# A Flamingo layer on one core: rows stored tile by tile on Pool, selection ahead of the row extreme, and half of the softmax exponentials straight from PSUM on ACT

## The reference, cut to what matters

```python
# x (2,1024,256), ctx (2,64,256); 16 heads of 64; 8 experts of width 192, top 2
q = einsum('bsd,dhf->bshf', layernorm(x), Wq) + bq;  q = q / sqrt(64)
k, v = ctx @ Wk + bk, ctx @ Wv + bv                  # 64 keys per batch
probs = softmax(einsum('bqhf,bkhf->bhqk', q, k), axis=-1)
x = x + tanh(g_xattn) * (einsum(probs, v) @ Wo + bo)
y = layernorm(x)
scores = sigmoid(y @ W_router)
_, sel = top_k(scores + expert_bias, 2)
w = scores[sel] / (sum + 1e-20)
out = silu(y @ Wg_s) * (y @ Wu_s) @ Wd_s             # shared expert
out += sum over the 2 chosen e of w_e * (silu(y @ Wg[e]) * (y @ Wu[e]) @ Wd[e])
x = x + tanh(g_ffn) * out
```

## Time and profile before

| | us |
|---|---|
| median of 3 runs | 340.79 |
| lowest, highest | 337.12, 341.66 |
| the profiled execution | 341.64 |
| its span in the trace | 339.9 |
| granted TensorE clock, mean | 0.925 |

### The profile page before, as it was taken

The page is one execution under the profiler, slowest core; times in us unless marked ns, Lnnn a source line. Parts: engine busy times, 40 slices in busy tenths (PEclk is TensorE's granted clock), DMA queues, the critical chain, the costliest instruction groups (busy, mean ns, idle before and its releaser), DMA issues.

```text
span 339.9 us, 6401 instructions
## 1 busy us (share of the span) xinstructions
PE 287.4 (85%) x1792; PEld 259.9 (76%) x1793; DVE 254.9 (75%) x672; ACT 143.3 (42%) x349; POOL 161.2 (47%) x208
## 2 busy tenths in 40 slices
PE   3968979999989989969678848798999999999660
PEld 2957768999978888959577748697898989999440
DVE  1687898999999998869785673269766667776586
ACT  1471653555655655635353323543344344444100
POOL 7022023356638888884876554029343434343400
PEclk9997998999999999979987996789999999999755
DMA  6790003011112222211100144023333343331768
GB/s 189 276 355 12 0 0 95 1 48 47 49 46 78 95 93 79 74 53 48 63 32 33 47 156 145 16 66 94 96 108 111 84 122 96 114 105 43 243 220 278
DMA packets 28892, 33.23 MB, mean 98 GB/s; under 512 B 3688, under 2 KB 25538, under 8 KB 28866
## 3 DMA queue, kind: packets, MB, share of 16 engines
q1 hardware_dynamic: 22706, 21.82, 21.5%
q0 software_dynamic: 3408, 8.46, 7.1%
q10 hardware_dynamic: 2752, 2.63, 2.4%
HBM read 21.14 MB, written 12.67 MB: 99 GB/s over the span
## 4 chain that ended last, share of the span: by engine, by line
PE 52%; DVE 21%; POOL 10%; issue 8%; ACT 3%; DMA 3%; SPq 1%; DVEq 0%; POOLq 0%; ACTq 0%
PE bank L1234 9%; PE bank L1236 8%; PE bank L1235 8%; PE scores_ps L1234 6%; PE scores_ps L1235 5%; PE scores_ps L1236 5%; POOL rows_dram L544 4%; DMA x_sb<-in_x_dram 3%; PE bank L1382 3%; POOL probs L573 2%; PE bank L1221 2%; DVE probs L1052 2%; DVE row_sum L1030 2%; DVE pT_lo L1025 2%; DVE x_sb L1144 2%
## 5 line engine op out<-in xcount | busy, mean ns | idle before, releaser
L624 POOL DMA_INDIRECT routed_dram<-probs,sct_idx x39 | 38.4, 986 | 68.8 <-DVE probs L1131 67.2
L1236 PE MATMUL bank<-AB_hi,pT_lo 128*128 128x256 f32 (+1 forms) x206 | 59.4, 289 | 0.0
L573 POOL TENSOR_TENSOR probs<-probs,row_inv 128x1024 f32<-128x1024 f32 x16 | 30.5, 1904 | 35.1 <-DVE row_inv L1034 35.1
L1236 PEld LDWEIGHTS bank<-AB_hi,pT_lo 128*128 128x128 f32 (+1 forms) x206 | 40.8, 198 | 0.0
L1234 PE MATMUL bank<-AB_hi,pT_hi 128*128 128x256 f32 x128 | 39.1, 306 | 0.0
L1235 PE MATMUL bank<-AB_lo,pT_hi 128*128 128x256 f32 x128 | 37.7, 295 | 0.0
L544 POOL DMA_INDIRECT rows_dram<-xn,slot_i x32 | 31.9, 996 | 11.3 <-issue 8.9
L1234 PE MATMUL scores_ps<-AB_hi,xnT_hi 128*128 128x512 f32 x64 | 26.4, 412 | 3.2 <-DVE xnT_lo L1014 3.2
L1234 PE MATMUL bank<-AB_hi,pT_lo 96*128 x78 | 25.2, 323 | 2.0 <-DVE pT_lo L1134 1.9
L1234 PEld LDWEIGHTS bank<-AB_hi,pT_hi 128*128 128x128 f32 x128 | 26.4, 206 | 0.1
L1235 PEld LDWEIGHTS bank<-AB_lo,pT_hi 128*128 128x128 f32 x128 | 26.1, 204 | 0.1
(11 more groups left out here) (222 smaller groups left out, 839.7 us busy)
## 6 DMA issues: line engine op xcount, KB each, us to landing
probs<-rows_dram SPq DMA_DIRECT2D x30, 130.0 KB, 2.2
x_sb<-in_x_dram SPq DMA_DIRECT2D x2, 1024.0 KB, 9.6
AB_free<-routed_dram SPq DMA_DIRECT2D x4, 512.0 KB, 5.6
AB_free<-routed_dram SPq DMA_DIRECT2D x8, 256.0 KB, 4.6
out_dram<-x_sb ACTq DMA_DIRECT2D x8, 256.0 KB, 2.2
raw_buf<-in_L_ffn_Wg_dram SPq DMA_DIRECT2D x8, 192.0 KB, 2.5
raw_buf<-in_L_ffn_Wu_dram SPq DMA_DIRECT2D x8, 192.0 KB, 3.0
raw_buf<-in_L_ffn_Wd_dram SPq DMA_DIRECT2D x4, 384.0 KB, 3.5
```

The source lines that it names most:

```text
L573: nc.gpsimd.tensor_tensor(pr, pr, row_inv[:, :].unsqueeze(2).to_broadcast([P, H, KV]), ALU.mult).then_inc(norm_done, 1)
L624: nc.gpsimd.indirect_dma_start(routed_dram[:, :], bass.IndirectOffsetOnAxis(ap=sct_idx[(k - 2) % (2 * RING)][:, 0:1], axis=0), y_sb[ks][:, ...
L1236: return nc.tensor.matmul(out_ap, a_lo, b_hi, start=False, stop=last)
```

## The change

Four things are edited.

1. POOL: `put_batch` with its table of parts becomes `put_tile(t)`, one tile (two indirect stores) a step from step 6 on, placed right after the second layernorm and **ahead of** the normalisation of the probabilities; steps 14 and 15 store two tiles each.
2. DVE: `choose` moves from behind the subtraction to in front of the row extreme.
3. The sign of the scores is turned in the folded weights, so that the row extreme is a minimum, `neg_max`. For heads 0 to 7, ACT now reads `scores_ps` itself, with `exp(-s + neg_max)`, one activation of 64 columns for each head, whose accumulator output gives that head's row sum (`direct_exponentials`, signal `direct_done`). Heads 8 to 15 keep the old way: subtraction on DVE (512 columns), exponential on ACT (512 columns), sum on DVE (512 columns). The next tile's scores wait for `direct_done` too.
4. ACT's list: the exponential stands behind `xnT_hi` in all steps, `W_hi` in front of `xn2T_hi`, and the eight new activations behind `xn2T_hi` and in front of `AB_hi`.

```diff
@@ POOL
-            def put_batch(b, part=slice(None)):
-
+            def put_tile(t):
+
+                b = [t < z for _, z in BATCHES].index(True)
                 pool.wait_ge(slot_done, b + 1)
                 pool.wait_ge(payload_done, b + 1)
-                for t in list(range(*BATCHES[b]))[part]:
-                    put_rows(t)
+                put_rows(t)
...
                 if inside(w):
                     second_norm(w)
+                if 6 <= t < T:
+                    put_tile(t - 6 if t < T - 2 else 2 * t - 20)
                 if inside(m):
...
-                if t == 6:
-                    put_batch(0, slice(0, 1))
-                if t == 7:
-                    put_batch(0, slice(1, 2))
-                if t == 8:
-                    put_batch(0, slice(2, 4))
...
-                if t == 12:
-                    put_batch(2, slice(0, 2))
...
+                if T - 2 <= t < T:
+                    put_tile(2 * t - 19)
@@ ACT
-                                         scale=DH ** -0.5, bias=q_beta[:, c:c + 1]).then_inc(wqT_done, 1)
+                                         scale=-DH ** -0.5, bias=q_beta[:, c:c + 1]).then_inc(wqT_done, 1)
...
                 def exponentials():
                     act.wait_ge(sub_done, m + 1)
-                    nc.scalar.activation(prob[1 - q][:, :], prob[1 - q][:, :], ACT.Exp).then_inc(exp_done, 1)
-
-                if inside(m) and not scores_first:
-                    exponentials()
+                    nc.scalar.activation(prob[1 - q][:, HK // 2:], prob[1 - q][:, HK // 2:], ACT.Exp, scale=-1.0).then_inc(exp_done, 1)
+
+                def direct_exponentials():
+                    act.wait_ge(max_done, u + 1)
+                    after(act, pT_done, 2 * t + 2)
+                    for h in range(H // 2):
+                        heads = slice(h * KV, (h + 1) * KV)
+                        e = nc.scalar.activation(prob[q][:, heads], scores_ps[:, heads], ACT.Exp, scale=-1.0,
+                                                 bias=neg_max[:, h:h + 1], accum_out=row_sum[:, h:h + 1])
+                    e.then_inc(direct_done, 1)
+
                 if inside(u):
...
+                if inside(m) and not scores_first:
+                    exponentials()
                 if folding:
...
                 if inside(w):
                     second_norm(w)
-                    high_xn2(w, 1 - q)
                 if 2 <= t < 2 + E:
...
+                if inside(w):
+                    high_xn2(w, 1 - q)
+                if inside(u):
+                    direct_exponentials()
                 if 2 + E <= t < 6 + E:
@@ DVE
-                    nc.vector.tensor_reduce(row_sum[:, :], prob[1 - q][:, :].rearrange("p (h k) -> p h k", k=KV),
+                    nc.vector.tensor_reduce(row_sum[:, H // 2:], prob[1 - q][:, HK // 2:].rearrange("p (h k) -> p h k", k=KV),
                                             AX_X, ALU.add).then_inc(sum_done, 1)
                     dve.wait_ge(sum_done, m + 1)
+                    dve.wait_ge(direct_done, m + 1)
...
+                for b, (_, z) in enumerate(BATCHES):
+                    if z + 1 == t:
+                        choose(b)
                 if inside(u):
 
                     dve.wait_ge(scores_done, u + 1)
                     after(dve, sub_done, u)
-                    nc.vector.tensor_reduce(row_max[:, :], sc, AX_X, ALU.max).then_inc(max_done, 1)
+                    after(dve, direct_done, u)
+                    nc.vector.tensor_reduce(neg_max[:, :], sc, AX_X, ALU.min).then_inc(max_done, 1)
...
-                for b, (_, z) in enumerate(BATCHES):
-                    if z + 1 == t:
-                        choose(b)
                 if inside(t):
                     second_norm(t)
@@ PE
                     pe.wait_ge(xT_lo_done, u + 1)
                     after(pe, sub_done, u)
+                    after(pe, direct_done, u)
```

More of the change, by code:

```diff
@@ L101, in flamingo_layer @@
         kT = [pr[:, :].rearrange("p (c h s) -> p c h s", h=2, s=P) for pr in prob]
-        row_max = sb("row_max", [P, H])
+        neg_max = sb("neg_max", [P, H])
         row_sum = sb("row_sum", [P, H])
@@ L294, in flamingo_layer @@
         exp_done = sem("exp_done")
+        direct_done = sem("direct_done")
         sum_done = sem("sum_done")
@@ L587, in step @@
                                             Wd_hi[:, part, :].bitcast(F32), ALU.subtract).then_inc(wd_lo_done, 1)
-                if t == 6:
-                    put_batch(0, slice(0, 1))
-                if t == 7:
-                    put_batch(0, slice(1, 2))
-                if t == 8:
-                    put_batch(0, slice(2, 4))
-                if t == 9:
-                    put_batch(1, slice(0, 1))
-                if t == 10:
-                    put_batch(1, slice(1, 3))
-                if t == 12:
-                    put_batch(2, slice(0, 2))
-                if t == 13:
-                    put_batch(2, slice(2, 3))
-                if t == 14:
-                    put_batch(3, slice(0, 1))
-                if t == 15:
-                    put_batch(3, slice(1, 2))
+                if T - 2 <= t < T:
+                    put_tile(2 * t - 19)
             token_loop(step, between)
             second_norm(T - 1)
-            put_batch(4)
-            put_batch(5)
+            for t in range(BATCHES[4][0], T):
+                put_tile(t)
             def late_add(z):
@@ L810, in _ @@
             nc.vector.tensor_copy(ctxT[:, :, :], bank[0][:, 0:KC * P].rearrange("p (k s) -> p k s", k=KC)).then_inc(ctxT_done, 1)
-            nc.vector.tensor_scalar(bias_cols[:, 0:HP], bank[0][:, 256:256 + HP], DH ** -0.5 / D, None, ALU.mult).then_inc(ctxT_done, 1)
+            nc.vector.tensor_scalar(bias_cols[:, 0:HP], bank[0][:, 256:256 + HP], -DH ** -0.5 / D, None, ALU.mult).then_inc(ctxT_done, 1)
             nc.vector.tensor_copy(bias_cols[:, HP:3 * HP], bank[0][:, 256 + HP:256 + 3 * HP]).then_inc(ctxT_done, 1)
@@ L821, in _ @@
                 nc.vector.scalar_tensor_tensor(out=q_beta[:, 2 * j:2 * j + 2], in0=q_sum[:, 2 * j:2 * j + 2],
-                                               scalar=-DH ** -0.5 / D, in1=bias_cols[:, 2 * j:2 * j + 2],
+                                               scalar=DH ** -0.5 / D, in1=bias_cols[:, 2 * j:2 * j + 2],
                                                op0=ALU.mult, op1=ALU.add).then_inc(q_beta_done, 1)
@@ L1051, in step @@
                     after(dve, pT_done, 2 * t + 2)
-                    nc.vector.tensor_tensor(prob[q][:, :].rearrange("p (h k) -> p h k", k=KV), sc,
-                                            row_max[:, :].unsqueeze(2).to_broadcast([P, H, KV]),
+                    nc.vector.tensor_tensor(prob[q][:, HK // 2:].rearrange("p (h k) -> p h k", k=KV), sc[:, H // 2:, :],
+                                            neg_max[:, H // 2:].unsqueeze(2).to_broadcast([P, H // 2, KV]),
                                             ALU.subtract).then_inc(sub_done, 1)
-                for b, (_, z) in enumerate(BATCHES):
-                    if z + 1 == t:
-                        choose(b)
                 if inside(t):
```

## The result

| | before | after |
|---|---|---|
| median, us | 341.23 (4 runs) | 349.68 (4 runs) |
| lowest, highest | 337.12, 343.35 | 346.9, 350.2 |
| profiled execution, its span | 341.64, 339.9 | 350.18, 348.4 |

The ratio is 1.0272, with a 95% interval of 1.0158 to 1.0386: the changed kernel is slower by 1.6 to 3.9%, which is 5 to 13 us. Forecast were 345 us and +4.3; measured were 349.7 and +8.5.

What follows compares the result with a forecast made beforehand. PE bounds plain steps at 7.98 us, so only its waits could change: they sum to +4.6, the last tile's statistics come 5.0 later, less 0.7 for the clock gives +4.3, 345 us; range 333 to 357.

Steps and rivals of the forecast that it cites:

- slow rival: ACT: a head costs 0.33 us or more, so every step lengthens; 350 to 360 us, chance 0.34.
- a head's price, turning point: ACT: each direct exponential costs 0.30 us; above 0.326 its loop outlasts PE's plain step of 7.98 us.
- stores alone: POOL: by the walk, the new stores alone bring the end 3.9 us forward.
- plain steps, halves of DVE's work: Halved subtraction and sum save DVE 1.1 us a step, but PE is the bound: worth 0 in plain steps.
- start, at the row extreme of step 4: Loop start: scores wait behind the activations, 3.6 us instead of 1.65; with half a microsecond in the next step, +2.0.
- first selection and step 6, to step 7: PE's waits around the first selection and step 6 were to grow from 1.8 to 2.9 us.
- steps 8 to 10, second selection, to step 9: PE's waits in steps 8 to 10 were to fall from 2.4 to 1.9 us.
- steps 10 to 15, to the last statistics: PE's waits in steps 10 to 15 were to grow from 12.3 to 14.3 us.
- clock: PE's clock: two long waits are left of four, so less time at the low level; 0.7 us taken off.
- the length of the selection: DVE: the selection moved in front of the row extreme was to take 2.69 us, as in the old profile.
- Pool's part as a rival: Steps 10 to 13: POOL's round of 8.3 us against 7.98 becomes the bound; 1.2 us more, 346; no separate chance.
- The wait moves, it doesn't go: At the selections the 1.58 us `mask` wait goes; PE's transpose of `xn` waits 1.3 us instead, scores another 0.3.

Runs made afterwards that it cites:

- e1: The changed kernel with two one-input tensor_reduce in place of the selection's two two-input tensor_tensor: 345.11 us, +4.6 against the kernel before.
- e9: e7 with three more activations of 32 columns per step on ACT, results unused, ahead of the eight: 345.23 us, +5.7 against the kernel before.
- e3: The kernel before with the new stores alone (`put_tile` in place of `put_batch`): 336.35 us, -4.1.
- e10: e7 with direct exponentials only from tile 2 on, tiles 0 and 1 going the old way: 335.71 us, -3.8 against the kernel before.
- e2: The changed kernel with the selection put back behind the subtraction: 337.84 us, -2.6 against the kernel before.
- e7: e2 with the two one-input reduces of e1 in the selection: 339.37 us, -0.6 against the kernel before.
- e8: e3 with the two one-input reduces of e1 in the selection: 334.61 us, -5.3 against the kernel before.
- e5: e4 with the two one-input reduces of e1 in the selection: 337.92 us, -2.0 against the kernel before.
- e6: The kernel before with direct exponentials and ACT's new order alone, that is e2 with the old batched stores: 352.19 us, +12.2.
- e4: The changed kernel without direct exponentials, all 16 heads subtracted and summed on DVE, one exponential on ACT: 351.1 us, +10.6 against the kernel before.
- e12: e11 without its tensor_scalar, leaving four small unused DVE instructions: 341.1 us, +0.8 against the kernel before.
- e11: e8 with five small unused DVE instructions of 4 elements in steps 3 to 5, ahead of the subtraction: 340.94 us, timed once.

## Why the prediction was right in its range and wrong in the place

The time lies in the range (333 to 357), 4.7 us over the forecast. It lies where the slow rival put it, but not by that rival's mechanism: a head costs 0.29 us, not 0.33, and plain steps didn't lengthen. So that the range held it is partly luck: its upper part was there for a rival that did not come true, and the measured loss is twice the forecast one. The last column is e1, the changed kernel without the held instruction.

| step of the prediction | forecast | shown | in e1 |
|---|---|---|---|
| a head's price, turning point | 0.30; 0.326 | 0.29; e9 agrees with the loop | |
| stores alone | -3.9 | -4.1 (e3) | |
| plain steps, halves of DVE's work | 0 | 7.98 us still | 7.98 |
| start, at the row extreme of step 4 | +2.0 | +3.4; taken away, 3.2 less in all (e10) | +1.6 |
| first selection and step 6, to step 7 | 1.8 to 2.9, +1.1 | +3.8 | +1.3 |
| steps 8 to 10, second selection, to step 9 | 2.4 to 1.9, -0.5 | +4.7 | +0.7 |
| steps 10 to 15, to the last statistics | 12.3 to 14.3, +2.0 | -0.8 | +0.2 |
| step 14, wait for `xn2` | over 4 | 4.38 | 4.4 |
| last tile's statistics | +5.0 | +11.1 | +3.8 |
| clock | -0.7 | mean to there 0.93, before 0.96: a loss | 0.97 |
| the whole, medians | +4.3 | +8.5 | +4.6 |

The four stretches are differences of times on DVE. The row extreme of steps 4, 7 and 9 starts at 84.74, 111.16 and 129.29 us before, at 88.14, 118.36 and 141.18 in the changed kernel, and at 86.35, 114.12 and 132.92 in e1; the last tile's statistics come at 190.81, 201.95 and 194.63.

**The step that failed** is the length of the selection: "It takes 98.02 - 95.33 = 2.69 us". I took it from rows in which POOL was idle while the instruction with two inputs ran, and moved it 2.6 us ahead, to where POOL normalises and forms `W_lo`. There it takes 3.88 us, and in step 8 4.75; with the reduces of e1 it takes 2.67 and 2.37 at the same places. The waits of PE that I had as 1.3 us became 2.5 and 3.4, and behind both stands the low clock (0.50 and 0.52), where e1, with waits of 1.30 and 0.99, has 1.00. That turned the term of -0.7 into a loss.

With the held instruction gone (e1) the kernel stands at +4.6 against the kernel before, beside a forecast of +4.3. The total agrees better than its terms do, which is luck again: steps 10 to 15 were to cost 2.0 us of waits, and came to -0.8 in the changed kernel and +0.2 in e1. The waits are there (10.7 us for `xn2`, in both), but of the three low spells that the kernel before has in these steps one is left in the changed kernel. The term of the start has a slip of its own (1.95 and 0.5 for the next step are 2.4, not 2.0), and part of what it shows is not the change: e1, with the same lists up to there, has PEclk 0.94 from 53 to 57 us, the changed kernel 0.50, so the length of that low spell differs from run to run.

**Pool's part as a rival** was priced at 1.2 us, by its own round. It isn't the bound; it costs as the engine that DVE waits for.

**"The wait moves, it doesn't go"** named the right place, but too cheaply in words. The text gave the moved selection no sum of its own. Measured, with direct exponentials, the place costs 7.3 us (e1 less e2; 5.2 by e1 less e7). By the loop's arithmetic it lengthens the very loop in which they left 0.2 us of room; that this is the reason is argued, not tested alone. Without them, the selection in front and ACT's order together are 3.3 us over e8 (e5).

The direct exponentials, ACT's order included, cost 1.5 us where the stores are new and the selection is behind (e2 less e3), or 4.8 by e7 less e8, both with the reduces; most of it at the start (e10). ACT's new order was never run alone; its share in these numbers stays open. So does why the clock was higher between the last statistics and the first experts' stores in the changed kernel's profiled run.

## What to carry to other kernels

A duration read from one place holds only beside the same neighbours. Before a step is moved on DVE, look at what POOL does at the new place, and at which of the moved instructions read two SBUF operands; then put one operand in PSUM or use a reduce. Parts of a change don't add where they stand in one loop that is nearly full. The stores were worth -4.1 us alone and -14.8 beside the direct exponentials (e2 less e6); these cost 12.2 us with the old stores and 1.5 to 4.8 with the new. So a part is priced in the company in which it will run.

## What the runs showed of the hardware that I had not expected

- A DVE `tensor_tensor` of 3 elements a partition took 2.56 us (2.82 at most, in e4), with both inputs in SBUF and POOL at work; a reduce of the same values took 0.17 (e1). It may start under one POOL instruction and wait for the next as well (after, 127.77; e4 three times), if that follows at once.
- A float32 `tensor_tensor` of 4 elements is held too when both inputs are in SBUF (1.69 us, e12), and not when one is in PSUM (0.15). So integer inputs are not what it takes.
- A float32 `tensor_scalar` of 4 elements from SBUF to SBUF is held in the same way (1.76 us, e11).
- An activation with an accumulator output is two instructions, 0.20 and 0.09 us from start to start at 64 columns: 0.29 a head.
- Held time can cost more than itself where PE waits behind it: 8.4 us in four instructions made 12.6 us of the kernel's time (e4 less e5), with the granted clock at 0.50 in windows that follow. 3.6 us in two made some 3.8 (the changed kernel less e1, across turns).
